# Another order of the operations in the software pipeline on four engines: attention with decay, then a routed expert layer, one Trainium2 core

## The chip, the cores and the metric

One core of one Trainium2 chip runs the whole program. The metric is the time of the kernel on the device in microseconds (us). Three runs of the kernel before gave 884.71, 891.51 and 884.67 us; the median is 884.71.

## The reference

The input is 32 sequences of 256 tokens with 128 channels, f32. Two blocks follow one another, each with a residual and a layer norm behind it.

```
x = layernorm(x + attn(x))
x = layernorm(x + ffn(x))

attn: delta = shift(h) - h
      mus   = tanh(tanh((h + delta*mu) @ w1) @ w2 + b) mixed by x_out_w, + x_bias   (5 mixes: r, w, k, v, g)
      r, k, v, g = (h + delta*mu_i) @ w_i;   wd = exp(-exp(tanh((h + delta*mu_w) @ w_w1) @ w_w2 + w_b))
      per step:  o_t = r_t . S + (r_t*bonus*k_t).sum * v_t ;   S = S*wd_t + k_t (x) v_t
      o = groupnorm(o)*gn_weight + gn_bias, times silu(g), @ o_w
ffn:  shared = relu(x@w1+b1)@w2+b2
      logits = x@router_w + expert_bias; the best 2 of 16 experts, softmax over the two
      routed = sum of the weighted results of the two experts of each token
```

## The kernel before

**Tiling.** Two sequences (512 tokens) are a unit; there are 16 units. A first part (about the first 520 us) takes the units through attention, the first layer norm, the routing and the shared expert, and writes each token's row into the buffer of its two experts by indirect DMA. A second part runs the experts over tiles of 256 rows, and a third adds up and normalizes. The change touches the first part alone.

**The software pipeline.** Each of TensorE (PE), ScalarE (ACT), GpSimd (POOL) and VectorE (DVE) has its own `body(at)`: a list of operations, each with a distance `d`. `pipeline(body)` calls the list once in each round `i` and runs an operation for unit `i + d`, if there is such a unit. Each engine runs its own list in order, and waits for the others by semaphores (`done`: the unit's value must be there; `before`: the former unit's buffer must have been read). An instruction that waits holds up all behind it on its engine. Nothing plans the order: the lists are written out by hand.

**What the operations are.** `a_...` is the input side of attention for a unit (the mixes, r, w, k, v, g). `b_level` 0 to 4 (L443) are five levels of small matmuls of K against R; between level j and level j+1 stands POOL's `b_step` j (L926 to L939), which multiplies K and R by decays, so level 4 waits for `b_step` 3. `b_pair` (L1058, L1070) takes a level's result out of PSUM with a mask. `b_o_near` (L475), `b_k_tok` (L451), `b_kv` (L463) and `b_o_far` (L485) make the output from `pair`, K, V and the running state (`b_state`, L1077). `c_...` is what follows: group norm (`c_var`, `c_o_rstd`, `c_norm`, `c_turned`, `c_aff` at L773, `c_gated`), `c_attn` (L497), the residual and layer norm (`c_z`, `c_bn`, `c_rstd`, `c_shift`, `c_x1` at L785, `c_rows1` at L790), and the routing: `c_turn` (L503), `c_x1T` (L796), `c_logits` (PE L511, ACT L802, DVE L1148), `c_top`, `c_chosen`, `c_seen` (L1155 to L1175), `c_place` (PE L518 and L519, DVE L1180), `c_slots` (L1215 to L1229), `c_scatter` (POOL L959, indirect DMAs, two for each of four blocks of 128 tokens). `f_...` is the shared expert: `f_up` 0 to 3 (L541), each waiting for the ACT's `f_hid` (L812) of the one before since they share a PSUM bank, then `f_down` (L548) and `f_base` (L1237).

**Waits that matter below.** PE's `a_mix_k_v` (L332) waits for ACT's exp_w (L703), since it overwrites the bank that `a_w` (L384) wrote. PE's `a_v` (L407) waits for ACT's copy of K (`a_k` on ACT, L715), for the same reason. `b_kv` waits for ACT's `k_tok` (L748). `a_k` and `a_mix_g` wait for DVE's mixes (L1034 multiplies, L1045 adds). POOL's `c_scatter` 0 waits for `c_slots`. In the trace L323 is `by_seq`, which serves `a_decay_hid`, `a_r` and `a_k`; L939 is the end of a `b_step`, L946 is `c_o_rstd`, L952 is `c_rstd`.

Of the kernel before, what the change touches and what calls it, by code (L numbers as in the profile page):

```python
# [19 lines left out]
UNITS = SEQS // UB  # L20
# [39 lines left out]
def build(nc, hidden, hidden_t, mats_dram, cols_dram, masks_dram, w1_dram, w2_dram, b2_dram, out):  # L60
# [8 lines left out]
    with ctx:  # L69
# [148 lines left out]
        def pipeline(body):  # L218
            for i in range(-4, UNITS + 3):
                def at(d, op, *args):  # L220
                    if 0 <= i + d < UNITS:
                        op(i + d, *args)
                body(at)
# [92 lines left out]
        def _(pe):  # L316
# [236 lines left out]
            def body(at):  # L553
                at(0, f_up, 0)
                at(2, b_o_near)
                at(2, b_k_tok)
                at(3, a_mix_k_v)
                at(2, b_kv)
                at(0, f_up, 1)
                at(0, c_place)  # L560
                at(3, a_k)
                at(3, a_mix_g)
                at(3, a_v)
                at(0, f_up, 2)
                at(2, b_o_far)
                at(3, a_g)
                at(1, c_attn)
                at(3, b_level, 1)
                at(3, b_level, 0)
                at(4, a_adapt0)  # L570
                at(0, f_up, 3)
                at(4, a_adapt1)
                at(3, b_level, 2)
                at(0, f_down, 0)
                at(4, a_mix_w_r)
                at(3, b_level, 3)
                at(0, f_down, 1)
                at(1, c_turn)
                at(4, a_decay_hid)
                at(4, a_r)  # L580
                at(1, c_logits)
                at(3, b_level, 4)
                at(4, a_w)
# [66 lines left out]
        def _(act):  # L650
# [163 lines left out]
            def body(at):  # L814
                at(0, b_o)
                at(1, a_g)
                at(1, a_v)
                at(2, a_adapt0)
                at(-2, f_hid, 3)
                at(2, a_adapt1a)  # L820
                at(2, a_adapt1b)
# [3 lines left out]
                at(2, a_decay_hid)  # L825
                at(-1, c_logits)
                at(2, a_r)
                at(2, a_w)
                at(-1, f_hid, 0)
                at(1, b_k_tok)  # L830
                at(1, b_chunk_decay)
                at(2, a_r_near)
                at(-1, f_hid, 1)
                at(2, a_k)
                at(-1, c_rows1)
                at(2, a_k_near)
                at(2, a_decay)
                at(-1, c_top_exp)
                at(0, c_aff)
                at(-1, f_hid, 2)  # L840
# [46 lines left out]
        def _(pool):  # L887
# [74 lines left out]
            def body(at):  # L962
                at(3, b_step, 3)
                at(3, b_step, 4)
                at(2, c_o_rstd)
# [458 lines left out]
```

## Time and profile before

| | |
|---|---|
| median of 3 runs | 884.71 us |
| the profiled execution's own time | 889.28 us |
| its span | 887.3 us |
| mean granted TensorE clock | 0.948 |
| PE busy | 788.1 us (89%) |
| DVE, ACT, POOL busy | 471.9, 484.1, 552.4 us |
| PE's share of the chain of waits | 72% (POOL 8%, DVE 4%, ACT 3%) |

```
## 2 busy tenths in 40 slices
PE   4788899999999999999977759999999999999492
PEld 1354455555665656555555449999999999988340
DVE  2435877777777777687754523333333333223076
ACT  2344666656656656566643306666666666546247
POOL 5435678878887888788876634555555555455344
PEclk9977999999999999999999969999999999999796
```

A slice is 22.2 us; each digit is the busy share in tenths. The first part is slices 1 to 24, and from slice 5 to slice 20 it runs evenly, a unit each 28 to 29.4 us. The experts start near 520 us. A busy PE is not PE at its peak, for matmuls are pipelined and their ends are modelled.

### The profile page before, as it was taken

To read this page: it belongs to the slowest core of one execution; us is meant where nothing else is said; L and a number is where in the kernel's file an instruction comes from. 1 tells how busy PE (TensorE), PEld (TensorE's weight loads), DVE (VectorE), ACT (ScalarE), POOL (GpSimd) and SP (SyncE) were. 2 spreads that over 40 slices of the span, in tenths; PEclk is the share of its full clock that TensorE was granted. 3 is DMA by queue.
4 is the path that set the end of the run, shared out by engine and by line. 5 is a ranking of instruction groups with operands and counts; after the bars stand their busy time and mean duration, and the time that the engine had idled before them with its cause. 6 is when DMAs were issued, how large, how long until landed. Compare 5 with 4: busy or idle time off the path is not lost.

```text
span 887.3 us, 24076 instructions
## 1 busy us (share of the span) xinstructions
PE 788.1 (89%) x8042; PEld 569.7 (64%) x8043; DVE 471.9 (53%) x1381; ACT 484.1 (55%) x1147; POOL 552.4 (62%) x691
## 2 busy tenths in 40 slices
PE   4788899999999999999977759999999999999492
PEld 1354455555665656555555449999999999988340
DVE  2435877777777777687754523333333333223076
ACT  2344666656656656566643306666666666546247
POOL 5435678878887888788876634555555555455344
PEclk9977999999999999999999969999999999999796
DMA  4000112202221122211113521222222222222394
GB/s 165 13 26 2 44 54 64 64 24 62 57 67 43 43 59 63 61 41 48 47 41 91 210 69 45 73 71 67 72 70 65 66 66 62 63 61 52 113 314 142
DMA packets 70324, 63.44 MB, mean 71 GB/s; under 512 B 8002, under 2 KB 61640, under 8 KB 70112
## 3 DMA queue, kind: packets, MB, share of 16 engines
q1 hardware_dynamic: 60816, 44.99, 17.9%
q0 software_dynamic: 9152, 17.07, 5.9%
q8 instruction: 52, 0.85, 0.4%
q14 instruction: 32, 0.26, 0.1%
q10 hardware_dynamic: 272, 0.26, 0.1%
HBM read 38.75 MB, written 25.50 MB: 72 GB/s over the span
## 4 chain that ended last, share of the span: by engine, by line
PE 72%; POOL 8%; issue 7%; DVE 4%; ACT 3%; DMA 2%; another core or an unknown queue 2%; SPq 0%; POOLq 0%; ACTq 0%; DVEq 0%
PE psO L616 16%; PE psB L605 15%; PE psO L541 6%; PE psP L332 5%; PE psB L485 4%; POOL w_ring L939 3%; PE psB L443 3%; POOL dispatched_rows L959 3%; PE psP L407 2%; PE psP L323 2%; PE psO L548 2%; PE psP L596 2%; PE psB L475 2%; PE psP L347 2%
## 5 line engine op out<-in xcount | busy, mean ns | idle before, releaser
L982 POOL DMA_INDIRECT expert_results<-yw_all,rows x158 | 155.5, 984 | 155.8 <-ACT yw_all L857 126.9
L616 PEld LDWEIGHTS psO<-w_sb,hide 128*128 128x128 f32 x1264 | 152.9, 192 | 6.7 <-issue 2.9
L616 PE MATMUL psO<-w_sb,hide 128*128 x1264 | 154.5, 275 | 1.0 <-ACT hide L849 1.0
L849 ACT ACTIVATE hide<-psB,w_ring 128x256 f32<-128x256 f32 x316 | 123.8, 475 | 56.0 <-PE psB L605 53.8
L959 POOL DMA_INDIRECT dispatched_rows<-rows,slot x128 | 130.8, 1022 | 35.0 <-issue 31.0
L605 PE MATMUL psB<-x1T,w_ring 128*128 128x256 f32 x632 | 151.3, 383 | 0.6 <-DVE x1T L1283 0.3
L1296 DVE TENSOR_TENSOR K<-psO,b_sb 128x256 f32<-128x256 f32 x79 | 33.6, 425 | 171.4 <-PE psO L616 138.2
L605 PEld LDWEIGHTS psB<-x1T,w_ring 128*128 128x128 f32 x632 | 114.9, 192 | 14.4 <-issue 1.7
L939 POOL TENSOR_TENSOR w_ring<-w_ring,tot 128x128 f32<-128x128 f32 (+2 forms) x160 | 117.9, 759 | 0.0
L857 ACT ACTIVATE yw_all<-K,rows 128x128 f32<-128x128 f32 x158 | 54.8, 395 | 78.5 <-issue 47.1
L1034 DVE SCALAR_TENSOR_TENSOR psP<-psP,cols,delta 128x512 f32<-128x512 f32 x80 | 57.3, 754 | 72.2 <-PE psP L332 72.2
L926 POOL TENSOR_TENSOR tot<-tot 128x128 f32<-128x128 f32 (+4 forms) x80 | 21.5, 269 | 95.3 <-PE psB L443 37.9
L541 PE MATMUL psO<-x1T,mats 128*128 128x512 f32 x128 | 75.4, 673 | 2.4 <-ACT hide L812 2.4
L812 ACT ACTIVATE hide<-psO,cols 128x512 f32<-128x512 f32 x64 | 44.1, 689 | 58.4 <-PE psO L541 56.0
L548 PE MATMUL psO<-mats,hide 128*128 128x128 f32 x512 | 68.0, 289 | 5.6 <-ACT hide L812 5.6
L548 PEld LDWEIGHTS psO<-mats,hide 128*128 128x128 f32 x512 | 62.4, 200 | 11.7 <-ACT hide L812 9.3
L1045 DVE TENSOR_TENSOR mixed<-psP,hT 128x512 f32<-128x512 f32 x80 | 52.0, 684 | 2.1
L1290 DVE COPY w_ring<-w_sb 128x516 f32 x79 | 33.9, 430 | 30.5 <-issue 30.5
L946 POOL TENSOR_TENSOR o_rstd<-o_var,minus_half 128x16 f32<-128x16 f32 x16 | 46.9, 2932 | 1.0 <-DVE o_var L1086 1.0
L332 PE MATMUL psP<-adapt1a,mats 32*128 32x512 f32 x128 | 39.3, 691 | 5.9 <-ACT adapt1b L672 4.7
L443 PEld LDWEIGHTS psB<-w_ring,K 64*32 64x32 f32 x2048 | 20.2, 109 | 36.3 <-issue 35.0
L878 ACT ACTIVATE w_sb<-hide,delta 128x128 f32<-128x128 f32 x64 | 25.9, 481 | 28.9 <-DVE delta L1344 23.0
(172 smaller groups left out, 1302.0 us busy)
## 6 DMA issues: line engine op xcount, KB each, us to landing
rows<-dispatched_rows SPq DMA_DIRECT2D x80, 132.0 KB
w_sb<-expert_results SPq DMA_DIRECT2D x8, 1024.0 KB, 11.9
h_res<-in_hidden SPq DMA_DIRECT2D x16, 256.0 KB, 3.0
out<-w_sb SPq DMA_DIRECT2D x16, 256.0 KB, 2.3
hT<-in_hidden_t SPq DMA_DIRECT2D x15, 256.0 KB, 4.5
w_sb<-in_w SPq DMA_DIRECT2D x14, 256.0 KB
expert_results<-yw_all,rows POOLq DMA_INDIRECT x158
dispatched_rows<-pad_rows SPq DMA_DIRECT2D x17, 132.0 KB
```

What stands on the lines that cost most here:

```text
L332: mm(ps, w, a, start=True, stop=True, **kw).then_inc(sem(f"mix_ps{n}"))
L541: mm(O1, mat("shared_w1")[:, c * 128:(c + 1) * 128], x1T[u % 2][:, :], start=True, stop=True).then_inc(sem(f"hid_ps{c}"))
L548: last = mm(O1[:, j * 128:(j + 1) * 128], hid[:, c, j * 128:(j + 1) * 128], mat("shared_w2")[:, c * 128:(c + 1) * 128], start=(c == 0), st ...
L605: last = mm(up_ps(p)[:, c // 2, (c % 2) * ST:(c % 2 + 1) * ST], w1b[i % W_RING][:, c * 128:(c + 1) * 128], xTe[p], start=True, stop=True)
L616: last = mm(psO[:, p, s * 128:(s + 1) * 128], hide[p][:, c, s * 128:(s + 1) * 128], w2_sb[:, bass.ds(e, 1), c, :].rearrange("p e c -> p (e ...
L849: last = A(hide[p][:, c, :], psB[:, 2 * p + c // 2, (c % 2) * ST:(c % 2 + 1) * ST], ACT.Relu, bias=w1b[i % W_RING][:, HIDDEN + c:HIDDEN + ...
L857: last = A(yw[i][:, s, :], ye[p][:, s, :], ACT.Copy, scale=row_in[i][:, s, AT_W:AT_W + 1])
L939: last = G.tensor_tensor(r, r, l, ALU.mult)
L959: G.indirect_dma_start(rows_dram[:, :], bass.IndirectOffsetOnAxis(slot[u % 2][:, j, k:k + 1], 0), rows[k][u % 2][:, j, :], None).then_inc( ...
L982: G.indirect_dma_start(back_dram[:, :], bass.IndirectOffsetOnAxis(row_in[i][:, s, AT_DEST:AT_DEST + 1].bitcast(u32), 0), yw[i][:, s, :], N ...
L1034: V.scalar_tensor_tensor(ps, ps, col(f"x_bias{n}"), delta[:, :, :], ALU.add, ALU.mult).then_inc(sem(f"mul{n}"))
L1045: V.tensor_tensor(mixed[MIX_BUF[n]][:, :, :], unflat(psP[MIX_BANK[n]]), hT[u % 2][:, :, 1:T + 1], ALU.add).then_inc(sem(f"mixed{n}"))
```

## The change

Only the lists and the bounds of the rounds change; no operation is added, removed or altered. The rounds run from -3 to UNITS+3 instead of -4 to UNITS+2, and the distances are moved with them. Read as one endless sequence, with the distances put on a common base, each engine meets the same units side by side as before, and this is what differs:

- **POOL**: nothing. Its list is the same sequence, cut at another place (`b_step` 3 ends the round instead of starting it).
- **PE**: before `a_r, c_logits, b_level 4, a_w, f_up 0, b_o_near, b_k_tok, a_mix_k_v, b_kv, f_up 1, c_place, a_k, a_mix_g, a_v, f_up 2, b_o_far`; after `a_r, b_level 4, c_logits, f_up 0, a_w, b_o_near, a_mix_k_v, b_k_tok, f_up 1, c_place, b_kv, a_k, a_mix_g, f_up 2, a_v, b_o_far`.
- **ACT**: before `c_logits, a_r, a_w, f_hid 0, b_k_tok, b_chunk_decay, a_r_near, f_hid 1, a_k, c_rows1, a_k_near, a_decay, c_top_exp, c_aff, f_hid 2, b_o`; after `a_r, c_logits, a_w, b_chunk_decay, c_rows1, f_hid 0, b_k_tok, f_hid 1, a_r_near, a_k, a_k_near, c_top_exp, a_decay, c_aff, b_o, f_hid 2`. `a_adapt1b` also goes ahead of `a_adapt1a`.
- **DVE**: before `b_pair 2, b_pair 3, c_var, f_base, c_logits, b_pair 4`, after `b_pair 2, c_var, f_base, b_pair 3, b_pair 4, c_logits`; before `b_state, c_norm, c_turned, c_place, a_mul G, a_add G, c_gated, c_slots, a_gate, c_z, c_bn, b_pair 0, a_delta, c_shift, b_pair 1`, after `c_norm, c_turned, b_state, a_mul G, c_place, a_add G, c_gated, a_gate, c_z, c_bn, b_pair 0, b_pair 1, a_delta, c_slots, c_shift`.

The diff, all of it:

```
--- before.py
+++ after.py
@@ -216,7 +216,7 @@
 
 
         def pipeline(body):
-            for i in range(-4, UNITS + 3):
+            for i in range(-3, UNITS + 4):
                 def at(d, op, *args):
                     if 0 <= i + d < UNITS:
                         op(i + d, *args)
@@ -551,36 +551,36 @@
                     last.then_inc(sem("down_ps"))
 
             def body(at):
-                at(0, f_up, 0)
-                at(2, b_o_near)
-                at(2, b_k_tok)
-                at(3, a_mix_k_v)
-                at(2, b_kv)
-                at(0, f_up, 1)
-                at(0, c_place)
-                at(3, a_k)
-                at(3, a_mix_g)
-                at(3, a_v)
-                at(0, f_up, 2)
-                at(2, b_o_far)
-                at(3, a_g)
-                at(1, c_attn)
-                at(3, b_level, 1)
-                at(3, b_level, 0)
-                at(4, a_adapt0)
-                at(0, f_up, 3)
-                at(4, a_adapt1)
-                at(3, b_level, 2)
-                at(0, f_down, 0)
-                at(4, a_mix_w_r)
-                at(3, b_level, 3)
-                at(0, f_down, 1)
-                at(1, c_turn)
-                at(4, a_decay_hid)
-                at(4, a_r)
-                at(1, c_logits)
-                at(3, b_level, 4)
-                at(4, a_w)
+                at(-1, c_attn)
+                at(1, b_level, 1)
+                at(1, b_level, 0)
+                at(2, a_adapt0)
+                at(-2, f_up, 3)
+                at(2, a_adapt1)
+                at(1, b_level, 2)
+                at(-2, f_down, 0)
+                at(2, a_mix_w_r)
+                at(1, b_level, 3)
+                at(-2, f_down, 1)
+                at(-1, c_turn)
+                at(2, a_decay_hid)
+                at(2, a_r)
+                at(1, b_level, 4)
+                at(-1, c_logits)
+                at(-1, f_up, 0)
+                at(2, a_w)
+                at(1, b_o_near)
+                at(2, a_mix_k_v)
+                at(1, b_k_tok)
+                at(-1, f_up, 1)
+                at(-1, c_place)
+                at(1, b_kv)
+                at(2, a_k)
+                at(2, a_mix_g)
+                at(-1, f_up, 2)
+                at(2, a_v)
+                at(1, b_o_far)
+                at(2, a_g)
 
             pipeline(body)
 
@@ -812,32 +812,32 @@
                 A(hid[:, c, :], O1, ACT.Relu, bias=col(f"shared_b1_{c}")).then_inc(sem(f"hid{c}"))
 
             def body(at):
+                at(1, a_decay)
+                at(-1, c_aff)
                 at(0, b_o)
+                at(-2, f_hid, 2)
                 at(1, a_g)
                 at(1, a_v)
                 at(2, a_adapt0)
                 at(-2, f_hid, 3)
+                at(2, a_adapt1b)
                 at(2, a_adapt1a)
-                at(2, a_adapt1b)
                 at(-1, c_x1)
                 at(0, c_sq)
                 at(-1, c_x1T)
                 at(2, a_decay_hid)
+                at(2, a_r)
                 at(-1, c_logits)
-                at(2, a_r)
                 at(2, a_w)
+                at(1, b_chunk_decay)
+                at(-1, c_rows1)
                 at(-1, f_hid, 0)
                 at(1, b_k_tok)
-                at(1, b_chunk_decay)
+                at(-1, f_hid, 1)
                 at(2, a_r_near)
-                at(-1, f_hid, 1)
                 at(2, a_k)
-                at(-1, c_rows1)
                 at(2, a_k_near)
-                at(2, a_decay)
                 at(-1, c_top_exp)
-                at(0, c_aff)
-                at(-1, f_hid, 2)
 
             pipeline(body)
 
@@ -960,17 +960,17 @@
                                          rows[k][u % 2][:, j, :], None).then_inc(sem(f"scattered{u % 2}"), 16)
 
             def body(at):
-                at(3, b_step, 3)
-                at(3, b_step, 4)
-                at(2, c_o_rstd)
-                at(0, c_scatter, 1)
-                at(0, c_scatter, 2)
-                at(4, b_step, 0)
-                at(0, c_scatter, 3)
-                at(4, b_step, 1)
-                at(2, c_rstd)
-                at(4, b_step, 2)
-                at(1, c_scatter, 0)
+                at(-1, b_step, 4)
+                at(-2, c_o_rstd)
+                at(-4, c_scatter, 1)
+                at(-4, c_scatter, 2)
+                at(0, b_step, 0)
+                at(-4, c_scatter, 3)
+                at(0, b_step, 1)
+                at(-2, c_rstd)
+                at(0, b_step, 2)
+                at(-3, c_scatter, 0)
+                at(0, b_step, 3)
 
             pipeline(body)
 
@@ -1238,38 +1238,38 @@
                                 rows[0][u % 2][:, :, 0:C], ALU.add).then_inc(sem("base_out"))
 
             def body(at):
-                at(0, b_pair, 2)
-                at(0, b_pair, 3)
-                at(-1, c_var)
-                at(-3, f_base)
-                at(-2, c_logits)
-                at(0, b_pair, 4)
-                at(-2, c_top)
-                at(-2, c_chosen)
-                at(-2, c_seen)
-                at(1, a_mul, MIX_K)
-                at(1, a_mul, MIX_V)
-                at(1, a_add, MIX_K)
-                at(1, a_add, MIX_V)
-                at(0, b_state)
-                at(-1, c_norm)
-                at(-1, c_turned)
-                at(-2, c_place)
-                at(1, a_mul, MIX_G)
-                at(1, a_add, MIX_G)
-                at(-1, c_gated)
-                at(-2, c_slots)
-                at(1, a_gate)
-                at(-1, c_z)
-                at(-1, c_bn)
-                at(1, b_pair, 0)
-                at(2, a_delta)
-                at(-1, c_shift)
-                at(1, b_pair, 1)
-                at(2, a_mul, MIX_W)
-                at(2, a_mul, MIX_R)
-                at(2, a_add, MIX_W)
-                at(2, a_add, MIX_R)
+                at(0, c_var)
+                at(-2, f_base)
+                at(1, b_pair, 3)
+                at(1, b_pair, 4)
+                at(-1, c_logits)
+                at(-1, c_top)
+                at(-1, c_chosen)
+                at(-1, c_seen)
+                at(2, a_mul, MIX_K)
+                at(2, a_mul, MIX_V)
+                at(2, a_add, MIX_K)
+                at(2, a_add, MIX_V)
+                at(0, c_norm)
+                at(0, c_turned)
+                at(1, b_state)
+                at(2, a_mul, MIX_G)
+                at(-1, c_place)
+                at(2, a_add, MIX_G)
+                at(0, c_gated)
+                at(2, a_gate)
+                at(0, c_z)
+                at(0, c_bn)
+                at(2, b_pair, 0)
+                at(2, b_pair, 1)
+                at(3, a_delta)
+                at(-1, c_slots)
+                at(0, c_shift)
+                at(3, a_mul, MIX_W)
+                at(3, a_mul, MIX_R)
+                at(3, a_add, MIX_W)
+                at(3, a_add, MIX_R)
+                at(2, b_pair, 2)
 
             pipeline(body)
 
```

## Rows read from the trace of the kernel before

**Rows 1.** Stretches: busy us and (instructions) per engine, then clock, DMA share, GB/s.

```profile
257.95:287.32 29.37, 27.91 (x373) 17.13 (x371) 21.00 (x60) 17.36 (x38) 23.15 (x31) 0.94 0.16 48
287.32:315.27 27.95, 26.63 (x373) 16.42 (x371) 21.68 (x61) 17.48 (x38) 22.64 (x31) 1.00 0.22 60
...
275.70:279.10 3.40, 3.40 (x13) 1.90 (x14) 2.64 (x4) 1.88 (x7) 3.03 (x4) 0.50 0.15 45
```

**Rows 2.** Waits of PE, 110 to 450 us: total us, times, longest.

```profile
PE psP L407 <- issue: 9.0, 12, 0.8
```

**Rows 3.** Timeline of PE in one unit: start us, us, what, [idle before].

```profile
290.74 0.45 PE L443 MATMUL psB<-w_ring,K 64*32 64x64 f32 x32
...
293.01 0.60 PE L503 MATMUL psO<-mats,rows 128*128 128x128 f32 x4
...
294.56 0.46 PE L511 MATMUL psO<-x1T,mats 128*32 128x128 f32 x8
295.26 0.46 PE L443 MATMUL psB<-w_ring,K 64*32 64x64 f32 x32 [0.24 <-POOL w_ring L939]
295.65 0.65 PE L384 MATMUL psP<-decay_hid,mats 64*64 64x256 f32 x4
296.23 1.13 PE L541 MATMUL psO<-x1T,mats 128*128 128x512 f32 x2
297.28 1.08 PE L475 MATMUL psB<-w_sb,pair 128*32 128x128 f32 x32
298.29 0.44 PE L451 MATMUL psB<-mats,K 128*128 128x128 f32 x2
298.66 1.13 PE L332 MATMUL psP<-adapt1a,mats 32*128 32x512 f32 x4
299.72 1.08 PE L463 MATMUL psB<-w_sb,k_tok 128*32 128x128 f32 x32
300.73 1.12 PE L541 MATMUL psO<-x1T,mats 128*128 128x512 f32 x2
...
302.26 0.65 PE L323 MATMUL psP<-mixed,mats 128*64 128x256 f32 x4
...
304.70 1.13 PE L407 MATMUL psP<-v_wc,mixed 128*128 128x128 f32 x8 [0.74 <-issue]
...
306.62 1.76 PE L485 MATMUL psB<-state,w_ring 64*128 64x32 f32 x28
```

**Rows 4.** Timeline of ACT in the same unit.

```profile
288.67 1.63 ACT L785 ACTIVATE rows<-z,z_shift,z_rstd 128x128 f32<-128x128 f32 x4
...
300.01 0.79 ACT L697 ACTIVATE R_near<-w_ring,cols 128x512 f32<-128x512 f32 x1
302.72 0.69 ACT L812 ACTIVATE hide<-psO,cols 128x512 f32<-128x512 f32 x1 [1.92 <-PE psO L541]
304.22 0.38 ACT L715 ACTIVATE K<-psP 128x256 f32<-128x256 f32 x1 [0.82 <-issue]
```

**Rows 5.** Timeline of POOL in the same unit: ends of b_step 2, 3.

```profile
288.58 1.58 POOL L939 TENSOR_TENSOR w_ring<-w_ring,tot 128x128 f32<-128x128 f32 x4
...
293.90 1.22 POOL L939 TENSOR_TENSOR w_ring<-w_ring,tot 128x256 f32<-128x256 f32 x2
```

**Rows 6.** Timeline of DVE in the same unit.

```profile
298.88 0.33 DVE L1175 TENSOR_TENSOR_SCAN seen<-running,either 128x80 f32<-128x80 f32 x1
...
307.45 1.15 DVE L1215 TENSOR_TENSOR place_of<-chosen,place 128x128 f32<-128x128 f32 x1
```

**Rows 7.** Timeline of DVE as the first part drains.

```profile
494.11 0.28 DVE L1215 TENSOR_TENSOR place_of<-chosen,place 128x128 f32<-128x128 f32 x1
```

**Rows 8.** Timeline of PE as the first part drains.

```profile
472.93 1.76 PE L485 MATMUL psB<-state,w_ring 64*128 64x32 f32 x28
```

**Rows 9.** Timeline of ACT as the first part drains.

```profile
479.24 0.60 ACT L761 ACTIVATE o_sb<-psB 128x512 f32<-128x512 f32 x1 [5.43 <-remote]
```

**Rows 10.** Waits of PE, 20 to 110 us, as the pipeline fills.

```profile
PE psP L323 <- DVE mixed L1045: 8.4, 6, 2.2
```

## The prediction

> **What bounds the kernel now.** I read the page first: PE carries 72% of the chain of waits. Then the stretches: between 110 and 450 us twelve units pass, and a unit takes 27.95 us with PE busy for 26.63 of it; each third unit takes 29.37 us at a mean clock of 0.94, because for 3.4 us the granted clock is 0.50 (the lower level, 1.2 GHz) [rows 1]. So PE's work fills a unit except for 1.32 us. The list of waits and the timeline of PE say where those are: 0.74 to 0.8 us before `a_v` in every unit [rows 2, 3], 0.24 us before level 4 [rows 3], and the rest, 0.34 us, inside levels 1 and 0. DVE, ACT and POOL are busy for 21.7, 17.5 and 22.6 us of 27.95 [rows 1]. A new order can therefore give back at most 1.3 us a unit, some 16 us in twelve units, and a clock that never falls would add 4 x 1.42 = 5.7 us. What it can lose has no such limit.
>
> The sum is made against the profiled execution, 889.28 us; the median of the runs is 884.71, 4.57 us lower, and I carry the same difference over.
>
> **POOL.** Its sequence is the same, at no cost. It still sets the time of level 4: `b_step` 3 ends at 295.12 [rows 5], and level 4 starts at 295.26 [rows 3].
>
> **PE, level 4 ahead of the logits.** Before, PE was through with `a_r` at 294.56, did `c_logits` and waited 0.24 [rows 3]. Now it waits from 294.56 to 295.26, about 0.7 us, and does the logits behind level 4. I lose what used to cover the wait: starting level 4 (295.26), 0.39 us later (the step to 295.65 in [rows 3]) the logits, 0.46 more to 296.11, `f_up` 0 (step 1.05) to 297.16, `a_w` (step 0.58) to 297.74. Before, `b_o_near` started at 297.28, so PE is **0.46 us late** here.
>
> **PE, from there to `b_o_far`.** Before, 297.28 to 306.62, that is 9.34 us with 0.74 us of wait [rows 3]. The same operations without the wait take 8.60, so `b_o_far` starts at 306.34, **0.28 us early**, if none of the moved operations finds its input missing. Each is checked, with the steps of rows 3:
> - `b_o_near` 297.74 to 298.75, then `a_mix_k_v`. It needs exp_w. `a_w` ends near 297.81, ACT's exp_w then takes some 0.5 (an estimate between K's 0.38 on 256 columns and the 0.69 of 512 [rows 4]), so it is there at about 298.45: 0.3 us to spare.
> - `b_k_tok` 299.81, then `f_up` 1 at 300.18. It needs `f_hid` 0, which ACT now does behind `b_chunk_decay` (224 columns, some 0.3) and `c_rows1` (512 columns, some 0.5 when instructions follow each other): 298.4 + 0.8 + 0.69 [rows 4] = 299.9. 0.3 us to spare.
> - `c_place` at 301.14 needs `c_seen`. The logits reach DVE about 1.3 us later; before, `c_seen` ended at 299.21 [rows 6]. It ends at about 300.3, for the pair of level 4 has been done by then. 0.8 us to spare (301.14 less 300.3); DVE's mixes for K and V start 0.2 to 0.3 us later, which `a_k`, now behind `b_kv` at 302.72, doesn't notice.
> - `a_k` 302.72, `a_mix_g` 303.31, `f_up` 2 304.42, `a_v` 305.37. `f_up` 2 stands where the wait was. `a_v` needs ACT's K. Before, K started 1.31 us after the recorded end of `a_k` on PE (302.91 to 304.22), with ACT idle for 0.82 of it [rows 3, 4]; nothing in the profile says why. I take the same delay: `a_k` ends at 303.37, K runs from 304.68 to 305.06. 0.3 us to spare. ACT does `a_r_near` ahead of K now, two instructions of at most 0.79 us [rows 4]; `f_hid` 1 starts 0.87 us after the end of `f_up` 1 (301.85 to 302.72), by the same delay at 302.2, so `a_r_near` is over by 302.9 + 1.5 = 304.4.
>
> **PE behind that.** `b_o_far` needs `b_state`, which moves behind `c_norm` and `c_turned` and, as `b_kv` is 2 us later, ends at about 305, with over 1 us in hand. `a_g`, `c_attn` and the levels keep their order: no cost. The later `f_hid` 2 is hidden by `b_o` and used only 4 us later.
>
> **DVE, the slots behind `a_delta`.** They took the idle time before `a_gate`. Now they stand before `c_shift`, whose value ACT needs for `c_x1` and PE for `c_turn`; x1 comes 1 to 1.5 us later. Before, it was done at 290.30 [rows 4] and used by `c_turn` at 293.01 [rows 3]: 2.7 us in hand. POOL's `c_scatter` 0 comes behind `b_step` 2, later than the slots. A term of zero.
> What a row shows of it: the first slot instruction, with two inputs in SBUF, took 1.15 us beside POOL's `b_step` 0 [rows 6] and 0.28 when POOL computed nothing [rows 7]. The Trainium skill, "SBUF — State Buffer", section "SBUF: two separate sides", says that a DVE instruction with two SBUF inputs and a POOL instruction that reads SBUF lock each other out for a whole instruction; the trace agrees (1.15 against 0.28). That speaks against this change, because the slots and the shift now meet `b_step` 2, on which level 3 waits. From the rows, holding POOL up by the instructions with two inputs (0.28, and two of about 0.16) makes `b_step` 2 end 0.6 us late. It ended at 290.16 [rows 5] and level 3 began at 290.74 [rows 3], so it is in hand, and the term is 0; all five small ones in the way, 1 us, would make it 0.4 us a unit, 5 us in all, the upper end.
>
> **Sum.** Twelve units x -0.28 = -3.4 us. While the pipeline fills, PE waited 8.4 us in six waits for DVE's mixes [rows 10], and `a_mix_k_v` ahead of `b_k_tok` starts each chain of K 0.37 us sooner: two units, -0.7. The drain has the same chains, 0 (between -0.5 and +1). Together -4.1: the profiled time becomes 885.2, the median **880.6 us**.
>
> **Rivals.**
> - *The clock never falls in the even stretch.* In the slow unit it fell from 275.70 to 279.10 [rows 1], right behind the wait before `a_v`; that wait goes, which speaks for it. Against it: a wait of 0.7 us arises before level 4. It gives -4.1 - 5.7 = -9.8: 874.9. Chance 0.15.
> - *The clock falls at the new wait, in every unit.* 12 falls instead of 4, each 1.42 us: +11.4 - 4.1 = +7.3, 892.0. It decides from where PE's gap at level 4 does what the 0.74 us gap did; against it, that one did so only in each third unit. Chance 0.12. The Trainium skill, "TensorE: Matmul & The Clock Gate", section "What's actually happening", makes the clock a matter of how busy PE has just been, at either of two levels; rows 1 agree (0.50 and 1.00), and it leaves open which of these two cases comes.
> - *K comes late, slower.* The place is ACT's K before `a_v`. Small matmuls are followed by late news on other engines: `b_o_far` ends at 474.69 [rows 8], and ACT's `b_o` starts at 479.24 after idling 5.43 us [rows 9], while POOL was sending its indirect DMAs. `b_kv` now stands right ahead of `a_k`, amid such DMAs. From a delay of 1.6 us on `a_k` (1.31 + 0.3) every further 0.1 is lost: at 2.6 us a unit costs 1.0 more, +12 - 4.1: 892.6 (the bottom of this case; two in three of it lie above); at the 4.55 of the drain (474.69 to 479.24) 2.95 more, +35 - 4.1 = 916. Against it: 1.31 is what it is now, also with DMAs about. Chance 0.20.
> - *Nothing is left of the gain.* The four margins of 0.3 us are each half used up, or a wait inside the levels grows: 884.7, within 3 us; with 5 us for `b_step` 2 besides it is 890. Chance 0.15.
>
> **Numbers.** The forecast has 0.38. The range reaches from just under the clock rival, 873, to 898, over the lower part of the K rival; under 873 and over 898 I leave about 0.17. A measurement of this kernel can tell 1%, 8.8 us, from no change. Faster by over 1% (under 875.9): 0.13 of the first rival's 0.15 and 0.04 of the forecast's, 0.17. Slower (over 893.6): 0.15 of the K rival, 0.05 of the second clock rival and 0.05 of the last, for several margins that go at once, 0.25. Within: 0.58.
>
> **What would show it.** In the profile after: no wait before L407; a wait of about 0.7 us before level 4 (L443, released by POOL's L939) in each unit; units of 27.7 us; PE busy unchanged. L541 waiting for L812, or L332 for L703, refutes the margins of `f_hid` 0 and exp_w. L407 waiting over 0.3 us means that K is late. Granted clock over 110 to 450 us above or below 0.98 decides between the clock rivals. Slots late would show as POOL's L959 waiting for DVE, x1 late as L503 waiting for L785. The forecast is wrong if a unit takes over 28.4 us on average.

## The result and the profile after

The kernel after took 931.4, 938.43, 924.03 and 915.68 us, median **927.71**. Beside it the kernel before took 884.71, 891.51, 884.67 and 892.12, median 888.11. The ratio is 1.036, with a 95% interval from 1.023 to 1.048. Two of the runs after, 931.4 (the profiled one) and 938.43, were in a slower state with a lower mean clock; every ratio here leaves such runs out (without them the median is 919.86), so a ratio is not always the quotient of the two medians. The forecast was 880.6, within 1%; it is 47 us off and outside its range, 873 to 898. The execution that is profiled here has a span of 929.5 us. A later profile of the same kernel (s3, 916.37 us, span 914.4) shows the same waits (ACT's K 36.4 us in 11), and its units stand beside these below, because the profiled execution has more of the lower clock.

The stretches of the kernel after, three units from `a_g` to `a_g`, and one stretch inside the second and third, with the columns of [rows 1]:

```profile
265.03:295.65 30.62, 28.00 (x372) 17.34 (x370) 20.95 (x60) 17.77 (x38) 22.53 (x31) 0.95 0.17 50
295.65:328.59 32.94, 30.31 (x372) 19.57 (x370) 20.94 (x60) 17.71 (x38) 24.42 (x33) 0.86 0.16 46
328.59:361.06 32.47, 30.01 (x373) 19.29 (x371) 20.08 (x60) 17.75 (x38) 22.19 (x30) 0.87 0.17 47
...
322.73:332.97 10.24, 9.49 (x87) 7.97 (x95) 4.00 (x8) 5.51 (x12) 4.30 (x5) 0.50 0.05 15
```

A unit takes 32.01 us on average, against 28.42 (two of 27.95 and one of 29.37, [rows 1]): 3.59 more. PE idles for 2.57 of it instead of 1.36 (+1.21) and is busy for 29.44 instead of 27.06 (+2.38) with the same matmuls. The second part is the clock: it is at 0.50 for 10.24 us around one change of unit, and the mean of the three units is 0.89 instead of 0.98. The last `a_g` of the first part starts at 489.00 instead of 451.09:

```profile
489.00 2.07 PE L413 MATMUL psP<-mixed,mats 128*128 128x512 f32 x2
```

So 37.9 of the 42.1 us between the two profiled executions arise before it. The remaining 4.2 lie in the drain and in the experts, and I did not take them apart. Three units of s3:

```profile
261.27:291.45 30.18, 27.43 (x372) 16.92 (x370) 20.06 (x60) 17.48 (x38) 23.24 (x31) 0.98 0.18 50
291.45:323.56 32.11, 29.85 (x372) 18.92 (x371) 19.67 (x60) 17.50 (x38) 22.77 (x32) 0.87 0.17 47
323.56:353.93 30.37, 28.08 (x372) 17.48 (x370) 20.09 (x60) 17.72 (x38) 21.29 (x30) 0.93 0.18 50
```

They take 30.89 us on average, 2.46 more than before: +1.07 of idling and +1.39 of busy time. The idling has grown by about as much in both; the other 1 us of busy time a unit is lower clock that the profiled execution had beyond that. In s3 the last `a_g` starts at 476.48, and 25.4 of the 27.1 us to the profiled execution before arise ahead of it.

The waits of PE from 110 to 450 us, which answer to [rows 2], then those of ACT and DVE in the same stretch (total, times, longest):

```profile
PE psP L407 <- issue: 17.8, 10, 1.8
PE psB L443 <- POOL w_ring L939: 7.7, 11, 0.9
```

```profile
ACT K L715 <- remote: 34.1, 10, 3.5
```

```profile
DVE state L1077 <- remote: 25.1, 10, 2.9
```

The wait before `a_v` (L407) is not filled, it has grown from 0.75 us to 1.78 a unit, though `f_up` 2 now stands ahead of it. ACT's K waits 3.4 us in each unit and DVE's `b_state` 2.5, each for something that the profile can't name ("remote"). One unit on PE, which answers to [rows 3], with ACT's K and POOL's indirect DMAs:

```profile
280.92 0.70 PE L443 MATMUL psB<-w_ring,K 64*32 64x64 f32 x32 [0.86 <-POOL w_ring L939]
281.55 0.43 PE L511 MATMUL psO<-x1T,mats 128*32 128x128 f32 x8
281.90 1.13 PE L541 MATMUL psO<-x1T,mats 128*128 128x512 f32 x2
282.96 0.65 PE L384 MATMUL psP<-decay_hid,mats 64*64 64x256 f32 x4
283.54 1.08 PE L475 MATMUL psB<-w_sb,pair 128*32 128x128 f32 x32
284.55 1.13 PE L332 MATMUL psP<-adapt1a,mats 32*128 32x512 f32 x4
285.61 0.44 PE L451 MATMUL psB<-mats,K 128*128 128x128 f32 x2
285.88 1.02 PE L541 MATMUL psO<-x1T,mats 128*128 128x512 f32 x2
...
287.31 1.08 PE L463 MATMUL psB<-w_sb,k_tok 128*32 128x128 f32 x32
288.32 0.65 PE L323 MATMUL psP<-mixed,mats 128*64 128x256 f32 x4
288.90 1.12 PE L332 MATMUL psP<-adapt1b,mats 32*128 32x512 f32 x2
289.95 1.12 PE L541 MATMUL psO<-x1T,mats 128*128 128x512 f32 x2
292.83 1.13 PE L407 MATMUL psP<-v_wc,mixed 128*128 128x128 f32 x8 [1.75 <-issue]
```

```profile
288.21 0.76 ACT L697 ACTIVATE R_near<-w_ring,cols 128x512 f32<-128x512 f32 x1
292.35 0.38 ACT L715 ACTIVATE K<-psP 128x256 f32<-128x256 f32 x1 [3.38 <-remote]
```

```profile
286.47 1.06 POOL L959 DMA_INDIRECT dispatched_rows<-rows,slot  x1 [0.20 <-issue]
287.84 0.96 POOL L959 DMA_INDIRECT dispatched_rows<-rows,slot  x1 [0.30 <-issue]
289.10 0.96 POOL L959 DMA_INDIRECT dispatched_rows<-rows,slot  x1 [0.30 <-issue]
290.37 0.96 POOL L959 DMA_INDIRECT dispatched_rows<-rows,slot  x1 [0.30 <-issue]
```

`a_k` (L323) is over at 288.97 and ACT is free at that time, but K starts at 292.35, 3.38 us later; before it was 1.31 [rows 3, 4]. K starts about 1 us after the last of four indirect DMAs (291.33). DVE's `b_state` needs `b_kv` (L463), over at 288.39, and starts at 292.31, at the same time as K. So the ends of `b_kv` and `a_k` reach the other engines together, and late. In what follows the end of a PE operation is called "told" when its semaphore goes up in the trace; the times come from the trace's record of semaphore updates. In this unit `b_kv`, `a_k`, `a_mix_g` and `f_up` 2 end at 288.39, 288.97, 290.02 and 291.08 by the record, and are told at 292.19, 292.24, 292.29 and 292.33. The ends on PE are modelled, so PE itself might have been slow; but `f_up` 2 alone is 1 us of work, and it is told 0.04 us behind `a_mix_g`. So it is the telling that was held, not the work.

### The profile page after: what moved, and what is told of

It is laid out like the page before. It is cut to its first block, busy times and chain, and to the rows that moved or that the text cites. A ratio compares the mean times of both kernels' runs of the same rounds, so it can differ in the third digit from the quotient of the medians.

```text
span 929.5 us, 24076 instructions
## 1 busy us (share of the span) xinstructions
PE 815.5 (88%) x8042; PEld 595.6 (64%) x8043; DVE 458.2 (49%) x1381; ACT 487.5 (52%) x1147; POOL 546.5 (59%) x691
## 4 chain that ended last, share of the span: by engine, by line
PE 67%; POOL 9%; issue 9%; DVE 4%; another core or an unknown queue 3%; ACT 3%; DMA 2%; DVEq 1%; SPq 0%; POOLq 0%; ACTq 0%
PE psO L616 14%; PE psB L605 13%; PE psO L541 6%; PE psP L332 4%; PE psB L485 4%; POOL w_ring L939 4%; POOL dispatched_rows L959 3%; PE psB L443 3%; PE psP L413 3%; PE psP L407 3%; PE psO L497 2%; PE psP L323 2%; PE psB L475 2%; PE psB L463 2%
## 5 line engine op out<-in xcount | busy, mean ns | idle before, releaser
L959 POOL DMA_INDIRECT dispatched_rows<-rows,slot x128 | 127.1, 993 | 35.9 <-issue 32.9
L926 POOL TENSOR_TENSOR tot<-tot 128x128 f32<-128x128 f32 (+4 forms) x80 | 23.6, 295 | 139.8 <-ACT tot L709 59.3
L541 PE MATMUL psO<-x1T,mats 128*128 128x512 f32 x128 | 73.0, 653 | 4.7 <-ACT hide L812 2.6
L443 PE MATMUL psB<-w_ring,K 64*32 64x64 f32 x2048 | 32.5, 236 | 13.9 <-POOL w_ring L939 13.8
```

Of the source, the lines that this page charges most:

```text
L443: last = mm(to, k, r, start=True, stop=True, tile_position=(64 * b, 32 * c4))
L541: mm(O1, mat("shared_w1")[:, c * 128:(c + 1) * 128], x1T[u % 2][:, :], start=True, stop=True).then_inc(sem(f"hid_ps{c}"))
L959: G.indirect_dma_start(rows_dram[:, :], bass.IndirectOffsetOnAxis(slot[u % 2][:, j, k:k + 1], 0), rows[k][u % 2][:, j, :], None).then_inc( ...
```

## The experiments

My theory after the traces (theory 1 below): `b_kv` is a burst of 32 small matmuls, and it now runs amid POOL's run of four indirect DMAs; from there on what PE ends is told late, K and `b_state` wait, `a_v` waits for K, and the clock falls at that wait. Rivals: the new order loses by something else, as ACT's or DVE's lists; the DMAs alone, or any matmuls, bring the late telling.

**Several chips.** The experiments came to five chips of the same kind, and the kernel before took 886.95 us on the first, 858.19 and 858.17 on the next two, 879.23 and 879.81 on the last two. Each kernel is compared with before on its own chip. Each chip was used in one session only, so whether the level belongs to the chip or to its condition at that time is not known.

### First chip (before 886.95)

**e1: before, with `b_kv` moved alone.**
```
-                at(2, b_kv)
                 at(0, f_up, 1)
                 at(0, c_place)
+                at(2, b_kv)
                 at(3, a_k)
```


> The kernel before with one operation moved on one engine: b_kv on PE goes from ahead of f_up 1 to behind c_place, amid POOL's run of four indirect DMAs. Theory 1 (the end of b_kv is told to the other engines only when POOL's run of DMAs is over, and with it the ends of all that PE does behind it, so ACT's K comes 3.3 us late): nearly the whole loss comes back, 915 to 935 us, L407 waits over 1.5 us in each unit and the clock falls in each. Theory 2 (the loss is the wait of level 4 that the logits no longer cover, and the clock that falls on it): no change, 884 to 892. Theory 3 (K is late because ACT does a_r_near ahead of it): no change either.


947.05 us, ratio 1.066 (1.061 to 1.072). Waits of PE and ACT, 110 to 450 us, and the stretch of one unit:

```profile
PE psP L407 <- issue: 29.4, 10, 3.0
```

```profile
ACT K L715 <- remote: 47.7, 10, 4.8
```

```profile
277.29:311.16 33.87, 30.72 (x373) 19.16 (x371) 21.13 (x60) 17.44 (x38) 22.62 (x31) 0.85 0.15 45
```

One line, with ACT and DVE as before, brings the whole loss and more than theory 1 allowed (915 to 935). Theories 2 and 3 had no change here. So the place of `b_kv` is enough.

**e2: after, with `b_kv` back ahead of `f_up` 1.**
```
+                at(1, b_kv)
                 at(-1, f_up, 1)
                 at(-1, c_place)
-                at(1, b_kv)
```


> The changed kernel with b_kv on PE put ahead of f_up 1 again, everything else as changed. Theory 1: b_kv ends about 1 us after POOL's DMAs have begun instead of 1.9 us, so part of the delay stays (b_kv told 1 to 3 us late); 885 to 915, the wait before L407 under 1.8 us. Theory 2 and theory 3: 915 to 930, as the changed kernel.


915.02 us, ratio 1.031 (1.025 to 1.037). The total decides nothing: it lies where the ranges of theory 1 and of its rivals meet. The waits do: the one at L407 is nearly gone, as theory 1 alone had it (under 1.8 us). But the late telling now also takes in `f_up` 1 and `c_place`, which stand behind the burst (`b_kv` is told 2.9 us late and `f_up` 1 by 1.9), and PE has other waits, one of them for k_tok:

```profile
PE psB L463 <- ACT k_tok L748: 7.8, 11, 0.7
...
PE psP L407 <- issue: 2.2, 7, 0.3
```

```profile
ACT hide L812 <- remote: 46.9, 11, 4.3
```

The wait for k_tok, 0.7 us a unit, is not the late telling: `b_kv` now follows right behind `b_k_tok`, which the change had put behind `a_mix_k_v`. So e2 does not say how much of the loss is `b_kv`'s place.

**e3: after, with the DMAs 3 us earlier** (POOL's `c_o_rstd` behind `c_scatter` 1 and 2).
```
-                at(-2, c_o_rstd)
                 at(-4, c_scatter, 1)
                 at(-4, c_scatter, 2)
+                at(-2, c_o_rstd)
```


> The changed kernel with one operation moved on POOL alone: c_o_rstd (2.9 us) goes behind c_scatter 1 and 2, so the four DMAs start 3 us sooner and are nearly over when PE does b_kv. PE, ACT and DVE are as changed. Theory 1: b_kv is told at once or under 1 us late, no wait before L407, 880 to 900 (c_norm comes 3 us later, which costs up to 1 us a unit). Theory 2: 915 to 930. Theory 3: 915 to 930.


950.67 us, ratio 1.073 (1.066 to 1.080): the time was missed. `b_kv` is no longer held (told 0.03 us late), but the DMAs (from 288.48) now meet another burst of 32, `b_o_near` (L475, 288.48 to 289.56), and what follows it is told up to 3.7 us late, up to 294.45. ACT's k_tok stands idle for 3.92 us:

```profile
290.55 0.44 PE L451 MATMUL psB<-mats,K 128*128 128x128 f32 x2
295.04 1.93 PE L463 MATMUL psB<-w_sb,k_tok 128*32 128x128 f32 x32 [2.71 <-ACT k_tok L748]
```

```profile
294.45 0.45 ACT L748 ACTIVATE k_tok<-psB 128x128 f32<-128x128 f32 x2 [3.92 <-remote]
```

The hold goes where the DMAs go; it does not belong to `b_kv`. The forecast left out what the earlier DMAs would meet.

**e4: before, with `f_up` 2 ahead of `a_v`.**
```
+                at(0, f_up, 2)
                 at(3, a_v)
-                at(0, f_up, 2)
```


> The kernel before with f_up 2 on PE ahead of a_v, one of the moves of the change alone. My prediction's term: the wait of 0.74 us before L407 in twelve units is filled, -8.9 us, and the clock may not fall any more, up to -5.7: 874 to 880. Against it: the end of f_up 2 or of a_v is told late as well, or the wait goes to level 4: 884 to 890.


882.19 us, ratio 0.996 (0.994 to 0.999), between the two forecasts (874 to 880, 884 to 890). The wait before `a_v` is gone and so are the falls of the clock: all units take 27.9 us.

```profile
272.67:300.58 27.91, 26.92 (x372) 16.67 (x370) 21.54 (x62) 17.38 (x38) 23.11 (x31) 1.00 0.18 54
```

```profile
PE psB L443 <- issue: 9.0, 24, 0.5
```

The slow third unit (29.37) has become a plain one, but the plain ones have gained only 0.05: PE is busy 0.29 us longer, and inside levels 1 and 0 it now waits 9.0 us in 24 waits, where it waited 3.5 in 11 before: 0.46 more a unit. Together that is the 0.75 that stood before `a_v`.

### Second chip (before 858.19)

**e5: as e1, with two plain 128x128 matmuls in place of the 32 small ones.** The code has 16 small ones, which the trace records as 32, and the two plain ones as 4. The edit leaves out the product of K and V. Shortened, beside the move of e1:
```
-  for par, g: mm(to[32*g...], k_tok[...], v_diag[...], tile_position=(0, 32 * g))
+  mm(psB[:, 1, c2 * 128:(c2 + 1) * 128], k_tok[:, c2, 0, :], v_diag...)
```


> The kernel before with b_kv behind c_place, as in the first experiment, but b_kv's 16 small matmuls (32 columns of weights each) are replaced by 2 plain ones of 128x128 that fill the same bank; what they compute is not K times V. Waits and engines are the same. Theory 1a (what is held back behind an indirect DMA is a burst of small matmuls and what follows it): no hold, no wait before L407, 878 to 890. Theory 1b (any matmul that ends amid the run of DMAs behind an ACT or DVE wait is told late): 930 to 950, as in the first experiment.


**e6: e4, with `c_scatter` 0 moved on POOL as well.**
```
                 at(3, b_step, 3)
+                at(0, c_scatter, 0)
...
-                at(1, c_scatter, 0)
```


> The kernel before with f_up 2 ahead of a_v on PE, and on POOL c_scatter 0 moved from behind b_step 2 to behind b_step 3, so that level 3 does not fall into its DMAs. Theory 1: level 3 is told at once instead of 2.0 us late, b_step 3 starts 1 us after b_step 2 and ends about 2 us sooner, PE's wait of 0.24 us before level 4 goes; but level 4 now ends near the end of these DMAs and may be told late. 876 to 884. Without theory 1 nothing is won: b_step 4 would only wait: 882.


**e7: after, with PE's list of before** (the distances one lower, for the new bounds).

> The changed kernel with PE's order of before; ACT's and DVE's orders as changed. If all of the loss were PE's order: 884 to 890. Theory 1: ACT does f_hid 0 and k_tok about 1.6 us later, so PE's b_kv starts later, amid the DMAs, and f_up 1 or b_kv is told late: 900 to 925.


**e8: before, with the logits behind level 4 on PE.**
```
-                at(1, c_logits)
                 at(3, b_level, 4)
+                at(1, c_logits)
```


> The kernel before with one move on PE: c_logits behind level 4. My prediction's term: 0.46 us a unit, +5.5 us: 890 to 895. Theory 1 adds: everything up to b_kv ends 0.46 us later, so b_kv ends 0.7 us into the DMAs instead of 0.2; if the hold begins there, b_kv and what follows are told up to 4 us late: 900 to 930.


They took 867.63, 857.3, 860.6 and 855.94 us, with ratios of 1.006 (1.002 to 1.011), 1.001 (0.998 to 1.004), 1.004 (1.002 to 1.007) and 0.996 (0.994 to 0.999). None tells the theories apart, for on this chip nothing is told over 0.34 us late in the even stretch of any of them, amid DMAs or not. That itself had to be followed up. The move of e6 was not made again on a chip where ends are told late.

### Third chip (before 858.17)

**e9: the kernel after, unchanged.**

> The kernel after, word for word, timed once more beside the kernel before. So far the kernel before has shown two levels: about 887 us where ends on TensorE behind a burst of small matmuls were told late amid POOL's indirect DMAs, and 858.2 where nothing was told late. Theory 1 (the loss is that late telling, and what the clock adds to the waits): where before is near 887, after is 3 to 5% slower again (915 to 930), K waits over 2.5 us in each unit; where before is near 858, nothing of the loss is left and after lies within 1% (852 to 866), no wait before a_v over 0.5 us. Rival (the new order itself costs, by its waits or engines): slower by 3% or more at both levels.


857.34 us, ratio 0.999 (0.998 to 1.000). The same code as at the top of this section:

```profile
264.05:290.39 26.34, 26.09 (x373) 16.43 (x371) 20.45 (x60) 17.48 (x38) 22.64 (x31) 1.00 0.20 58
290.39:316.67 26.28, 26.07 (x373) 16.41 (x371) 20.41 (x60) 17.58 (x38) 22.56 (x31) 1.00 0.20 58
```

```profile
284.11 1.08 PE L463 MATMUL psB<-w_sb,k_tok 128*32 128x128 f32 x32
285.12 0.65 PE L323 MATMUL psP<-mixed,mats 128*64 128x256 f32 x4
...
287.71 1.05 PE L407 MATMUL psP<-v_wc,mixed 128*128 128x128 f32 x8
```

```profile
285.90 0.38 ACT L715 ACTIVATE K<-psP 128x256 f32<-128x256 f32 x1
```

`b_kv` runs amid the DMAs as before (its end is 1.93 us behind the start of the first, 1.90 in the kernel after and in s3), but `a_k` ends at 285.77 and K starts at 285.90, with no wait. `a_v` follows `f_up` 2 without a gap, as the forecast had it. POOL holds level 4 for 0.26 us a unit:

```profile
PE psB L443 <- POOL w_ring L939: 3.4, 13, 0.4
```

**e10: e1 again.**

> The kernel before with PE's b_kv moved from ahead of f_up 1 to behind c_place, the same as the first run of these. Theory 1: 6 to 7% slower where before is near 887, and at most 1% slower where before is near 858. Rival (b_kv's place costs by its input k_tok or by the pair it feeds): over 1% slower at both levels, with waits of PE for k_tok or of DVE for b_kv beyond 1 us in each unit.


859.04 us, ratio 1.002 (1.000 to 1.004); on the first chip the same code gave 1.066.

**e11: e5 again. e12: e7 again.**

> As the run before, b_kv behind c_place, but of two plain 128x128 matmuls instead of 32 small ones (it leaves out the product of K and V; everything else is done, on other numbers). Where before is near 887: if the late telling needs the burst of small matmuls, a_k's end is told in under 1.5 us, ACT's K waits under 1 us beyond before's and the time is within 1.5% of before (875 to 900); if any matmuls behind the start of the DMAs are told late, it is 5% slower or more, as with the small ones. Where before is near 858 it says nothing: within 1.5% by both.

> The kernel after with PE's list of before, ACT's and DVE's lists as after. Theory 1 (all of the loss comes from PE's list, by the place of b_kv amid the DMAs): within 1% of before at either level. Rival (a part of the loss comes from ACT's or DVE's new order, as K behind r_near): where before is near 887, 1.5% slower or more, with ACT's K or hide late by it.


868.74 us, ratio 0.999 (0.994 to 1.003), and 860.76 us, ratio 1.001 (0.998 to 1.005). Of the plain matmuls this says nothing, as expected where nothing is late.

### Fourth chip (before 879.23)

**s1: e5's kernel. s2: e7's kernel. s3: the kernel after.**

> The kernel before with PE's b_kv behind c_place and of two plain 128x128 matmuls instead of 32 small ones (it leaves out the product of K and V). Where before is near 887: if the late telling needs the burst of small matmuls, K waits under 1 us beyond before's and the time is within 1.5% of before; if any matmuls that run behind the start of the DMAs are told late, 5% slower or more, as the same move with the small ones was (1.066). Where before is near 858: within 1.5%.

> The kernel after with PE's list of before. Where before is near 887: within 1% of before if PE's list alone carries the loss, 1.5% slower or more if ACT's or DVE's new order has a part in it. Where before is near 858: within 1%.

> The kernel after. Where before is near 887: 3 to 5% slower, with ACT's K waiting over 2.5 us a unit. Where before is near 858: within 0.5% of before, as in the last run of it (0.9992).


s1: 884.77 us, ratio 1.004 (0.999 to 1.009). s2: 884.9, 1.005 (1.001 to 1.009). s3: 916.78, 1.041 (1.032 to 1.051). Here ends are told late again, and s3 loses what it lost at first. With plain matmuls the same place of `b_kv` costs at most 0.9%, though `b_kv` itself is 0.45 us shorter (the lines of s1 behind L459 are lower by 4):

```profile
294.25 0.63 PE L459 MATMUL psB<-w_sb,k_tok 128*128 128x128 f32 x4
295.18 0.65 PE L323 MATMUL psP<-mixed,mats 128*64 128x256 f32 x4 [0.30 <-DVE mixed L1041]
...
296.82 1.16 PE L407 MATMUL psP<-v_wc,mixed 128*128 128x128 f32 x8
```

```profile
295.95 0.38 ACT L711 ACTIVATE K<-psP 128x256 f32<-128x256 f32 x1 [1.19 <-PE psP L323]
```

```profile
293.70 1.06 POOL L955 DMA_INDIRECT dispatched_rows<-rows,slot  x1 [0.19 <-issue]
```

`a_k` ends at 295.83, 2.13 us behind the start of the first DMA, and K starts 0.12 us later. So it takes the burst, not just matmuls amid DMAs. That this very execution had the hold is seen at another burst of 32, level 3, which ends amid the two DMAs of `c_scatter` 0: it is told 1.95 us late in s1, 2.01 in before, 2.29 in after and 0.16 in e9. And s2 shows that ACT's and DVE's new lists cost 0.1 to 0.9%: nearly all of the loss is in PE's list.

**s4: before, with `f_up` 2 ahead of `a_v` (e4) and the logits behind level 4 (e8).** The edits are those two.

> The kernel before with two moves on PE that cost nothing amid the DMAs: f_up 2 ahead of a_v, and the logits behind level 4. Each alone gave 0.9964 (at the level of 887) and 0.9962 (at the level of 858). Theory: both fill waits that lie elsewhere, so together 0.990 to 0.997 at either level. Rival (in the unit PE's waits are no bound once POOL's steps are): 0.998 or more.


898.16 us, ratio 1.020 (1.011 to 1.029). Missed: two moves that gained 0.4% each, one at either level, together lose 1 to 3%. Level 4 now waits 0.52 us and everything from `a_w` to `a_k` comes 0.36 us later, while the DMAs stay. `b_kv` ends 0.57 us behind the start of the first DMA instead of 0.21, and is told 2.18 us late instead of 1.09; `f_up` 1 too, so `f_up` 2 waits for ACT's `f_hid` 1:

```profile
279.74 1.09 PE L541 MATMUL psO<-x1T,mats 128*128 128x512 f32 x2 [0.65 <-ACT hide L812]
```

### Fifth chip (before 879.81)

**s5: after, with `b_kv` ahead of `f_up` 1 (e2) and the logits ahead of level 4.**
```
                 at(2, a_r)
+                at(-1, c_logits)
                 at(1, b_level, 4)
-                at(-1, c_logits)
```


> The kernel after with two moves of PE's list undone: b_kv back ahead of f_up 1 and the logits back ahead of level 4. With b_kv alone undone it was 1.031 where before was 887. Theory 1 (both of PE's moves that put a matmul whose end is needed behind a burst cost, and nothing else does): 1.000 to 1.015 where before is 875 to 890, PE's wait for k_tok (0.6 us a unit) still there. Rival (the logits are not it, but f_up 2, a_mix_k_v or f_up 0): 1.025 to 1.035. Where before is near 858: 0.995 to 1.005 by both.


903.3 us, ratio 1.027 (1.022 to 1.032). Missed by theory 1 (1.000 to 1.015) and inside the rival's range: `b_kv` still ends 0.99 us behind the start of the first DMA, because it waits 0.7 us (7.8 in 11 waits) for ACT's k_tok, with `b_k_tok` now behind `a_mix_k_v`. So putting the logits back does not bring back the rest; `b_k_tok` behind `a_mix_k_v`, which the rival named, may have a part in it (the wait for k_tok speaks for it; no run shows it).

**s6: e4 again.**

> The kernel before with f_up 2 ahead of a_v, timed again. Theory: it fills the 0.74 us before a_v, 0.993 to 0.998 where before is 875 to 890 (0.9964 in its first run), no wait at L407; where before is near 858 there is next to no wait to fill, 0.997 to 1.002. Rival (the first gain was chance, the wait only moves): 0.999 or more where before is 875 to 890.


877.18 us, ratio 0.999 (0.996 to 1.001). The gain of e4 is not confirmed: 0.0 to 0.4%. No version beat both kernels by more than that.

### All of it in one table

Medians over 6 to 9 units between 200 and 420 us, read from the semaphore updates of each trace, in us.

| kernel | `b_kv` ends behind the first DMA's start | `b_kv` told late | `a_k` told late | ratio |
|---|---|---|---|---|
| before (the profile ahead of the change) | 0.21 | 1.09 | 1.22 | 1 |
| s2 | 0.21 | 1.05 | 1.12 | 1.005 |
| e4 | 0.21 | 1.10 | 1.22 | 0.996 |
| s4 | 0.57 | 2.18 | 2.23 | 1.020 |
| s5 | 0.99 | 2.47 | 2.53 | 1.027 |
| e2 | 1.35 | 2.89 | 2.33 | 1.031 |
| e1 | 1.74 | 3.23 | 3.40 | 1.066 |
| after | 1.90 | 3.81 | 3.28 | 1.036 |
| s3 (after, fourth chip) | 1.90 | 3.73 | 3.20 | 1.041 |
| s1 (plain `b_kv`) | 1.18 | 0.01 | 0.01 | 1.004 |
| e9 (after, third chip) | 1.93 | 0.04 | 0.02 | 0.999 |
| e10 (e1, third chip) | 1.73 | 0.04 | 0.02 | 1.002 |

On the chips with the hold, the later `b_kv` ends behind the start of the DMAs, the later it is told, and more than in step: from 0.21 to 1.90, 1.69 us, the telling goes from 1.30 to 5.71 us behind that start, 4.4 us. This is a row of one operation's places and not a rule for any burst: `b_o_near` in e3 ends only 1.08 us behind the start and is told as late as `b_kv` in after. Nor are ends always told together: in before `b_kv`, `f_up` 1, `c_place` and `a_k` are told one by one, 0.7 us apart (329.80, 330.53, 331.28, 332.04 in one unit), while the DMAs still run. In the kernel after, `f_up` 1 and `c_place`, which run amid the same DMAs but ahead of the burst, are told within 0.02 us.

## Why the prediction was wrong

**The step that failed** is this one: "`a_v` needs ACT's K. Before, K started 1.31 us after the recorded end of `a_k` on PE ...; nothing in the profile says why. I take the same delay". The delay depends on where `b_kv` ends against POOL's DMAs, and the change moves it by 1.69 us. The delay became 3.38 us. I had a margin of 0.3 us on it, so 1.8 us of wait a unit is what the K rival's own sum gives (3.38 less 1.6); L407 waited 1.78. In twelve units that is 21 us, and with -4.1 the rival would have given 902. It was named with the right place and a chance of 0.20, and it was the one that came; its own sum of the delay was sound, but it had no term for the clock.

**The clock.** The rest is the lower clock. I priced a fall in every unit at the new wait before level 4, and none at a late K. It came behind the latter: in the unit shown the granted clock is 1.00 from level 4 (280.92) past the wait that ends at 292.83, and falls at 295.4. From [rows 1], 3.40 us at the lower level cost 1.42 us, 0.42 for each us. The three units after have 20.7 us at it ((1 - 0.95) x 2 x 30.62 and so on), 6.9 a unit, so 2.9 against 0.5 before: +2.4, and PE's busy time grew by 2.38. In s3 the same sum gives 13.8 us, 4.6 a unit, 1.9 against 0.5: +1.4, and PE's busy time grew by 1.39. By the kernels, in the even stretch: without a wait before `a_v` (e4, s4, s1) no fall; at 0.75 us a unit one of 3.4 us in each third unit; at 1.68 (s3) one of 6.8 to 10.2 us in seven of twelve; at 1.78 (after) one of 3.4 to 10.2 us in nearly each; at 2.94 (e1) one of 3.4 to 13.7 us in each. But the length of this wait is not all that counts: s2, with 0.83 us there, has two falls in twelve units, s5, with 0.69, three, e2, with 0.2 there and 0.7 before `b_kv`, falls in half of its units, and e3, which waits 2.7 us before `b_kv` instead, in most. No run was made to separate them.

**Level 4 ahead of the logits.** Forecast 0.7 us of wait and PE 0.46 us late. After has 0.70 a unit (7.7 in 11), s3 0.55, s4 0.54, e9 0.26 on its faster chip. The size was about right. Part of it may be the same hold (argued, not run): `b_step` 3 waits for level 3, which is told 2 us late where before is near 880. The step was wrong in what it left out: s4 shows that 0.36 us of lateness ahead of the burst is not worth 0.36 but doubles the hold.

**The margins.** exp_w, `f_hid` 0, `c_seen` and the slots held: no wait of PE for any of them in the rows above. These steps were right. The term for the slots was zero, and nothing waits for them:

```profile
304.34 0.32 DVE L1215 TENSOR_TENSOR place_of<-chosen,place 128x128 f32<-128x128 f32 x1
```

```profile
304.06 0.45 POOL L926 TENSOR_TENSOR tot<-tot 128x32 f32<-128x32 f32 x1 [0.37 <-issue]
304.90 1.58 POOL L939 TENSOR_TENSOR w_ring<-w_ring,tot 128x128 f32<-128x128 f32 x4
306.65 1.06 POOL L959 DMA_INDIRECT dispatched_rows<-rows,slot  x1 [0.17 <-issue]
```

The slots do meet POOL's `b_step` 2, as the prediction feared: the step runs from 304.06 to 306.48, 2.42 us instead of the 2.16 before (288.00 to 290.16), and its first instruction takes 0.45 us where it took 0.24. That is 0.26 us late and not 0.6, and it stays in hand (level 3 starts at 306.80, without a wait). The first slot instruction takes 0.32 us beside that step, not the 1.15 beside `b_step` 0 [rows 6]. The Trainium skill, "SBUF — State Buffer", section "SBUF: two separate sides", has a DVE instruction with two SBUF inputs and a POOL instruction that reads SBUF lock each other out for a whole instruction. POOL's 0.45 against 0.24 goes that way (DVE's L1027, 303.70 to 304.41, was under way when it started), but the slot instruction's 0.32, against 0.27 where POOL computes nothing (336.83 in the same trace), does not show it. In s3 the slots of most units run ahead of the step, and its first instruction takes 0.24.

**The filled wait.** On the chips where nothing is told late (e9) the forecast's timeline holds: no wait before `a_v`, a wait at level 4. But with PE's list of before (e7) the wait before `a_v` is only 3.2 us in 12 there, so the gain is 0.1% (0 to 0.2) and not 0.5%. The 0.74 us that I meant to fill was for the most part itself this late telling (`a_k` told 1.22 us late in before, 0.02 in e7). I read the number and not its cause.

## What to carry to other kernels

A delay that the profile calls "issue" or "remote" and that nothing explains must not be carried over to a new order as a constant. Ask what ran on the other engines at that time, and what a shift against it would do; here a burst of small matmuls amid indirect DMAs. Put a burst, and what others wait for behind it, so that it ends ahead of the DMAs' start (starting it behind their end was not tried), and look at a wait's effect on the clock together with the wait.

## What the runs showed of the hardware

- On three of the five chips (before 879 to 887 us) the end of a burst of 32 small matmuls that runs amid POOL's indirect DMAs, and the ends of what PE does behind it, are told late: `b_kv` by 1.09 to 3.81 us, at the latest about 1 us behind the last DMA's end. Four matmul records of 128x128 in the same place are told at once (s1). Whether it is the number of the small ones, their 32 columns or their tile positions was not separated. That the hold goes with POOL's DMAs is shown by e3; what the two share is open. A run without the DMAs wasn't tried.
- On two chips (before 858 us) there is no such hold, and the same kernel is 2.4 to 3.3% faster (858.2 against 879.2 and 887.0). A unit of the kernel after takes 26.3 to 26.9 us there (e9) and 30.2 to 32.1 on the fourth chip (s3). A ratio found on one chip can be the chip's: the change is worth 1.036 to 1.041 on one kind and 0.999 on the other.
